# Attention of a four-layer gated block: negated score maxima added by an extra float32r pass

## The reference

```python
q = (target @ Wq.T + bq).reshape(B, L, H, D).transpose(0, 2, 1, 3)   # k, v alike, of the context
q = _apply_rope(q, cos_q, sin_q)
attn = jnp.einsum('bhld,bhkd->bhlk', q, k) * scale
attn = jnp.where(context_mask[:, None, None, :], attn, -jnp.inf)
attn = jax.nn.softmax(attn, axis=-1)
x = jnp.einsum('bhlk,bhkd->bhld', attn, v)
```

## Time and profile before

| | us |
|---|---|
| median of 3 runs | 832.74 (831.04 to 834.12) |
| the profiled execution: its own time | 834.48 |
| its span, first to last instruction | 832.7 |
| mean granted TensorE clock, share of full | 0.932 |
| TensorE matmul busy / weight loads | 694.4 / 413.5 |
| DVE / ACT / POOL busy | 475.5 / 329.4 / 245.0 |
| attention stage, first unit to last copy | 109.30 to 327.71 |

### The profile page before, as it was taken

The page is one execution under the profiler, slowest core; times in us unless marked ns, Lnnn a source line. Parts: engine busy times, 40 slices in busy tenths (PEclk is TensorE's granted clock), DMA queues, the critical chain, the costliest instruction groups (busy, mean ns, idle before and its releaser), DMA issues. The chain is left out here.

```text
span 832.7 us, 10715 instructions
## 1 busy us (share of the span) xinstructions
PE 694.4 (83%) x3613; PEld 413.5 (50%) x3632; DVE 475.5 (57%) x873; ACT 329.4 (40%) x584; POOL 245.0 (29%) x407
## 2 busy tenths in 40 slices
PE   3699869998998997855799999999488999975886
PEld 1377633333333332742455665656355767662554
DVE  3576668888888871643763113121437555456995
ACT  0167626677677676412341111141031120202565
POOL 2356530011011010353050001010103164347797
PEclk9699977999999999885899999999789998996999
DMA  5010000000000001930000000000100000000011
GB/s 186 13 32 25 13 7 0 2 1 0 1 1 1 1 1 71 394 155 0 1 1 0 1 1 0 0 0 1 13 1 0 1 1 1 1 0 0 20 38 45
DMA packets 14104, 21.45 MB, mean 26 GB/s; under 512 B 2160, under 2 KB 11504, under 8 KB 13296
## 3 DMA queue, kind: packets, MB, share of 16 engines
q1 hardware_dynamic: 13200, 20.34, 7.1%
q10 hardware_dynamic: 864, 0.59, 0.2%
HBM read 18.83 MB, written 2.10 MB: 25 GB/s over the span
## 5 line engine op out<-in xcount | busy, mean ns | idle before, releaser
L630 ACT ACTIVATE prob<-ps_s 128x512 f32<-128x512 f32 x256 | 133.9, 600 | 72.3 <-PE ps_s L518 71.6
L562 DVE TENSOR_REDUCE mx<-ps_f 128x2 f32<-128x1024 f32 x128 | 150.0, 1218 | 15.6 <-PE ps_f L498 8.1
L1038 DVE SCALAR_TENSOR_TENSOR qs<-ps_u,wmax,qs 128x512 f32<-128x512 f32 x40 | 29.7, 749 | 113.9 <-ACT qs L1000 113.8
L1000 ACT ACTIVATE qs<-ps_g,wmax 128x512 f32<-128x512 f32 x40 | 27.4, 687 | 144.1 <-PE ps_u L903 144.1
L916 PE MATMUL ps_yE<-down,qs 128*128 128x256 f32 x320 | 77.7, 387 | 7.9 <-DVE qs L1038 6.8
L518 PE MATMUL ps_s<-q_stacks,k_stacks 64*128 64x512 f32 x256 | 75.7, 425 | 10.2 <-ACT prob L630 9.1
L498 PE MATMUL ps_f<-k_stacks,q_stacks 64*128 64x512 f32 x256 | 64.9, 502 | 16.7 <-DVE q_stacks L581 9.7
L916 PEld LDWEIGHTS ps_yE<-down,qs 128*128 128x128 f32 x320 | 61.3, 193 | 22.0 <-DVE qs L1038 9.0
L527 PE MATMUL ps_o<-prob,vst 128*32 128x512 f32 x512 | 69.0, 612 | 0.0
L498 PEld LDWEIGHTS ps_f<-k_stacks,q_stacks 64*128 64x128 f32 x256 | 25.3, 194 | 72.7 <-issue 28.7
L599 POOL COPY vst<-va 128x272 f32<-128x272 f32 x16 | 6.8, 428 | 167.1 <-PE ps_o L527 167.1
(11 more groups left out here) (245 smaller groups left out, 1258.7 us busy)
## 6 DMA issues: line engine op xcount, KB each, us to landing
up<-in_up SPq DMA_DIRECT2D x10, 256.0 KB, 6.7
x<-in_x SPq DMA_DIRECT2D x4, 512.0 KB, 7.9
ctxT<-in_ctxT SPq DMA_DIRECT2D x16, 128.0 KB, 2.0
ks<-in_ctxTC SPq DMA_DIRECT2D x1, 2048.0 KB, 11.9
ks<-in_ctx SPq DMA_DIRECT2D x1, 2048.0 KB, 17.4
out<-x SPq DMA_DIRECT2D x16, 128.0 KB, 1.7
down<-in_down SPq DMA_DIRECT2D x1, 1280.0 KB, 5.7
ks<-in_wqv SPq DMA_DIRECT2D x1, 1024.0 KB, 20.7
```

The costliest lines, as they stand in the source:

```text
L562: dve.tensor_reduce(mx[:, f % 2, qt, 2 * pair:2 * pair + 2], ps_f[n % 2][:, :, :], AX_X, ALU.max).then_inc(used, 1)
L630: act.activation(prob[:, kt % 2, j, :], ps_s[n % 3][:, :], ACT.Exp, scale=SCALE)\
L1038: dve.scalar_tensor_tensor(out=h[:, k % 2, :], in0=ps_u[k % 2][:, :], scalar=wmax[:, 3, order[k], 1:2], in1=sg[:, k % 2, :], op0=ALU.mult, ...
```

## The change

The negated maxima no longer go into the query stack. A step's maxima, transposed, now take a place in the ring of three `ps_s` (a *slot*), and ACT copies them to a new tile `minus` (float32r). `mt` holds two heads' worth of rows: the two pairs of a step share one set of four transposes. Each score gets a pass of its own ahead (`lowered`, now a function of TensorE): a stationary `pick` with ones in the two rows of its pair's maxima, and `minus` as the moving operand, with start=True; the score then accumulates on it. The pass for score j + 1 is issued before score j. The ring counts 17 slots for a step, the maxima's ahead of tile 2. `split` moves from DVE to POOL and becomes three operations. Fourteen units run ahead instead of twelve. DVE keeps only the row maxima.

```diff
-def max_unit(f):
-
-    return UNITS + (UNITS + 1) * f + (MAX_AFTER if f < STEPS - 1 else 0)
-
-
-def score_unit(f, i):
-
-    if f == 0:
-        return i
-    return UNITS + (UNITS + 1) * (f - 1) + i + (1 if i >= MAX_AFTER else 0)
+def score_slot(s, kt, j):
+
+    added = kt // 2 if s + 1 < STEPS else 0
+    return 1 + (QT * G + 1) * s + G * kt + j + added
+
+
+def max_slot(f):
+
+    return score_slot(f - 1, 2, 0) - 1 if f else 0
...
-        mt = sb("mt", [P, 2, QT, G, ROWS], F32)
+        mt = sb("mt", [P, 2, QT, 2, ROWS], F32)
+        minus = sb("minus", [P, 2, S], F32R)
+        pick = sb("pick", [P, 2, P], F32R)
...
-            def first_scores(f, i):
-
-                n = score_unit(f, i)
+            def first_scores(n):
+
                 wait(pe, used, n - 1)
+                f, i = divmod(n, UNITS)
...
             def maxima(f):
 
-                n = max_unit(f)
+                n = max_slot(f)
                 pe.wait_ge(mt_ready, f + 1)
-                wait(pe, used, n - 1)
-                for pair in range(2):
-                    for qt in range(QT):
-                        last = pe.transpose(ps_f[n % 2][:, pair, qt * P:(qt + 1) * P],
-                                            mt[:, f % 2, qt, 2 * pair:2 * pair + 2, :]
-                                            .rearrange("p h r -> p (h r)"), id32)
-                last.then_inc(filled, 1)
+                wait(pe, slot_read, n - 2)
+                for qt in range(QT):
+                    last = pe.transpose(ps_s[n % 3][:, qt * P:(qt + 1) * P],
+                                        mt[:, f % 2, qt, :, :].rearrange("p h r -> p (h r)"), id32)
+                last.then_inc(slot_done, 1)
+
+            def lowered(s, kt, j):
+
+                n = score_slot(s, kt, j)
+                pair, h = divmod(j, 2)
+                if kt == 0 and j == 0:
+                    pe.wait_ge(slot_read, max_slot(s) + 1)
+                wait(pe, slot_read, n - 2)
+                pe.matmul(ps_s[n % 3][:, :], pick[rows(h), pair, :], minus[rows(h), s % 2, :], start=True, stop=False)
 
             def scores(s, kt, j):
-                n = s * 16 + kt * G + j
-                wait(pe, exp_done, n - 2)
+                n = score_slot(s, kt, j)
                 pair, h = divmod(j, 2)
                 pe.matmul(ps_s[n % 3][:, :], ks[rows(h), 2 * s + pair, kt * P:(kt + 1) * P],
-                          qs[rows(h), 2 * s + pair, :], start=True, stop=True).then_inc(s_done, 1)
+                          qs[rows(h), 2 * s + pair, :], start=False, stop=True).then_inc(slot_done, 1)
 
             def values(s, kt):
-                pe.wait_ge(exp_done, s * 16 + kt * G + G)
...
-            for i in range(UNITS):
-                first_scores(0, i)
-            for i in range(MAX_AFTER):
-                first_scores(1, i)
+            for n in range(UNITS + 2):
+                first_scores(n)
             maxima(0)
-            for i in range(MAX_AFTER, 4):
-                first_scores(1, i)
+            for n in range(UNITS + 2, LEAD):
+                first_scores(n)
+            pe.wait_ge(pick_preset, 5)
+            lowered(0, 0, 0)
             for s in range(STEPS):
-                ahead = [(s + 1, i) for i in range(4, UNITS)] + [(s + 2, i) for i in range(4)]
-                pe.wait_ge(used, max_unit(s) + 1)
                 for kt in range(QT):
-                    if kt == QT - 1 and s + 1 < STEPS:
-                        maxima(s + 1)
                     for half in range(2):
-                        f, i = ahead[2 * kt + half]
-                        if f < STEPS:
-                            first_scores(f, i)
+                        ahead = UNITS * s + LEAD + 2 * kt + half
+                        if ahead < UNITS * STEPS:
+                            first_scores(ahead)
+                        if kt == 2 and half == 0 and s + 1 < STEPS:
+                            maxima(s + 1)
                         for j in (2 * half, 2 * half + 1):
+                            then = (s * QT + kt) * G + j + 1
+                            if then < STEPS * QT * G:
+                                lowered(then // (QT * G), then // G % QT, then % G)
                             scores(s, kt, j)
                     if kt:
...
+            for n in range(UNITS * STEPS):
+                f, i = divmod(n, UNITS)
                 qt, pair = divmod(i, 2)
+                if i == 0:
+                    wait(dve, mt_ready, f - 1)
...
 
-            def split(f):
-
-                dve.wait_ge(used, score_unit(f, UNITS - 1) + 1)
-                if f > 1:
-                    dve.wait_ge(filled, max_unit(f - 2) + 1)
-                high, low = mt[:, f % 2, :, :, MAX_ROW], mt[:, f % 2, :, :, MAX_ROW + 1]
-                dve.tensor_scalar(high.bitcast(F32R), mx[:, f % 2, :, :], -1.0, None, ALU.mult).then_inc(mt_half, 1)
-                dve.wait_ge(mt_half, f + 1)
-                dve.scalar_tensor_tensor(out=low, in0=mx[:, f % 2, :, :], scalar=-1.0, in1=high, op0=ALU.mult,
-                                         op1=ALU.subtract).then_inc(mt_ready, 1)
-
-            def lowered(f):
-
-                n = max_unit(f)
-                dve.wait_ge(filled, n + 1)
-                own = qs[:, 2 * f:2 * f + 2, :]
-                dve.tensor_tensor(own, ps_f[n % 2][:, :, :], own.bitcast(F32), ALU.add).then_inc(used, 1)
-            dve.wait_ge(mt_preset, 1)
-            for f in range(STEPS):
-                for i in range(UNITS):
-                    if f and i == MAX_AFTER:
-                        lowered(f - 1)
-                    first_maxima(f, i)
-                split(f)
-            lowered(STEPS - 1)
...
             pool.memset(mt[:, :, :, :, :], 0.0).then_inc(mt_preset, 1)
+            pool.memset(pick[:, :, :].bitcast(F32), 0.0).then_inc(pick_preset, 1)
+            pool.wait_ge(pick_preset, 1)
+            for h in range(2):
+                for pair in range(2):
+                    at = ROWS * h + ROWS // 2 * pair
+                    pool.memset(pick[at:at + 2, pair, :].bitcast(F32), 1.0).then_inc(pick_preset, 1)
+                    pool.wait_ge(pick_preset, 2 + 2 * h + pair)
...
+            def split(f):
+
+                pool.wait_ge(used, UNITS * (f + 1))
+                if f > 1:
+                    pool.wait_ge(slot_done, max_slot(f - 2) + 1)
+                own = mt[:, f % 2, :, :, :].rearrange("p q h (a c) -> p q a h c", a=2)
+                high, low = own[:, :, :, :, 0], own[:, :, :, :, 1]
+                m = mx[:, f % 2, :, :].rearrange("p q (a h) -> p q a h", h=2)
+                pool.tensor_scalar(high.bitcast(F32R), m, -1.0, None, ALU.mult).then_inc(mt_half, 1)
+                pool.wait_ge(mt_half, 2 * f + 1)
+                pool.tensor_tensor(low, m, high, ALU.add).then_inc(mt_half, 1)
+                pool.wait_ge(mt_half, 2 * f + 2)
+                pool.tensor_scalar(low, low, -1.0, None, ALU.mult).then_inc(mt_ready, 1)
...
             pool.wait_ge(bp_in, 16)
+            split(0)
             for s in range(STEPS):
                 if s > 1:
                     stage_values(s, s % 2)
+                if s + 1 < STEPS:
+                    split(s + 1)
                 bias(s)
...
         def _(act):
+            def copy_maxima(f):
+                n = max_slot(f)
+                act.wait_ge(slot_done, n + 1)
+                if f > 1:
+                    act.wait_ge(slot_done, score_slot(f - 2, QT - 1, G - 1) + 1)
+                act.copy(minus[:, f % 2, :], ps_s[n % 3][:, :]).then_inc(slot_read, 1)
+
             def exps(s, kt):
+                wait(act, pv_done, s * QT + kt - 1)
                 for j in range(G):
-                    n = s * 16 + kt * G + j
-                    act.wait_ge(s_done, n + 1)
-                    if j == 0:
-                        wait(act, pv_done, s * QT + kt - 1)
+                    n = score_slot(s, kt, j)
+                    if kt == 2 and j == 0 and s + 1 < STEPS:
+                        copy_maxima(s + 1)
+                    act.wait_ge(slot_done, n + 1)
                     act.activation(prob[:, kt % 2, j, :], ps_s[n % 3][:, :], ACT.Exp, scale=SCALE)\
-                       .then_inc(exp_done, 1)
+                       .then_inc(slot_read, 1)
...
+            copy_maxima(0)
```

More of the change, by code:

```diff
@@ L56 @@
 MAX_ROW, MASK_ROW = 3 * HD, 3 * HD + 2
-UNITS, MAX_AFTER = 2 * QT, 2
+UNITS, LEAD = 2 * QT, 14
 SCALE = HD ** -0.5
@@ L478, in phase_attend @@
         filled, used = sem("filled"), sem("used")
-        mt_preset, mt_half, mt_ready = sem("mt_preset"), sem("mt_half"), sem("mt_ready")
-        s_done, exp_done, pv_done, o_copied = sem("s_done"), sem("exp_done"), sem("pv_done"), sem("o_copied")
+        mt_preset, mt_half, mt_ready, pick_preset = sem("mt_preset"), sem("mt_half"), sem("mt_ready"), sem("pick_preset")
+        slot_done, slot_read, pv_done, o_copied = sem("slot_done"), sem("slot_read"), sem("pv_done"), sem("o_copied")
         v_preset, v_ready = sem("v_preset"), sem("v_ready")
```

(25 more changed lines are left out.)

## The result

| | before | after |
|---|---|---|
| median, us | 831.89 | 878.51 |
| lowest to highest | 830.94 to 834.12 | 877.08 to 880.03 |
| ratio, 95% interval | | 1.0562 (1.0532 to 1.0592) |
| the profiled execution | 834.48 | 877.08 |
| its span | 832.7 | 875.2 |

The medians stand 46.6 apart, the profiled executions 42.6: the profiled one of before (834.48) lies above its four timed ones, that of after is the lowest of its four. The stage grew by 43.9, and the rest of the program, untouched, took 1.4 less in this pair of profiles. So the whole change is in the stage.

What follows compares the result with a forecast made beforehand. It took a loop of waits through ACT and TensorE, DVE outside it, to bound the kernel. Steady steps +32.1, end +4.9 and start -1.9 sum to +35.1, taking the median from 832.74 to 868 us, range 852 to 884.

Steps and rivals of the forecast that it cites:

- 14 steady steps: Attention stage, steady stretch: each step goes from 12.55 to 14.84 us, +32.1 us over 14 steps.
- start of the stage: Before the transposes of step 1: DVE's wait for POOL's zeroing goes, fewer units follow; -1.9 us, between -3 and 0.
- end of the stage: From the transposes of step 15 to the last copy's end: 20.8 us for 15.9, +4.9 us.
- The mechanism: Key tiles: passes hold scores and values one exponential longer; a plain tile's values start at 1.56, +0.49 us a tile.
- hop: Delay between engines: 0.1 us a tile of uncertainty, 6 us each way in the range.
- weights loaded ahead of a held pass: Held pairs on TensorE might start 0.1 us sooner, some 6 us less in all; 0 was taken.
- POOL's split: Three small operations a step on POOL, 0.7 to 2.0 us with hops; cost 0, up to 1 us a step if uncovered.
- The pair of pass and score: On TensorE, opposite row halves overlap, so pass plus score costs what a pair costs now, 0.23 us, not 0.47.
- Serial passes: Rival: pass and score don't overlap on TensorE, 0.47 us together; +30 us, giving 898; chance 6%.
- The clock: Rival: more frequent TensorE waits lower its clock; +48 us if half the tiles ran so, giving 916; chance 3%.
- A held pass that holds nobody: Rival: score 3 and values start while the next tile's pass waits, plain tiles keep 2.83 us; 821; chance 5%.
- No difference: Rival: the hold is partly hidden in time priced as serial, and DVE's relief pays the rest; chance 4%.

Runs made afterwards that it cites:

- b_held: Kernel before with one number changed: each score waits for one exponential more than its buffer asks, no passes; 862.5 us, ratio 1.0379.
- a_nopass: Changed kernel without the 256 pass matmuls, their waits kept on the scores, maxima not taken off; 894.2 and 899.5 us.
- a_ring4: Changed kernel with the first scores' PSUM in three single banks and a fourth place in the scores' ring, all passes kept; 846.6 us, ratio 1.0178.
- a_waits: Changed kernel with three waits put otherwise: ACT asks for values after the score, the maxima's copy not at all, tile 0's pass drops one; 870.4 us, ratio 1.0455.
- a_swap: Changed kernel with score j issued ahead of the pass for score j + 1; 869.5 us, ratio 1.0447.
- a_full: Changed kernel, passes kept, with four-place scores' ring, reordered waits, scores ahead of next passes, values and second unit ahead of fourth score; 832.2 us, ratio 0.9995.

## Why the prediction was right

Forecast 868 with 852 to 884, slower at 91%; measured 878.5, so the rise is 46.6 where 35 was forecast. Term by term, from the two profiles:

| term | predicted | measured |
|---|---|---|
| 14 steady steps | +32.1 | 215.97 - 175.71 = +40.3 |
| start of the stage | -1.9 | 24.26 - 26.77 = -2.5 |
| end of the stage | +4.9 | 22.09 - 15.93 = +6.2 |
| rest of the program | 0 | -1.4 |
| span | +35.1 | +42.5 |

*The mechanism* was right in each place: the hold at 0.65 for the first pass and 1.14 for the second, the values behind it, 1.83 ahead of the maxima. b_held, a_nopass's tiles and a_ring4 tell it from the price of the passes. The longer hold alone is 30 of the 46.6 (b_held). The rest of a step is read from the traces: of 15.41 less 14.31, 0.30 are the second waits (a_waits), and 0.75 the way of the maxima through the scores' ring and ACT, since tiles 1 and 2 together take 8.42 in a_waits and 7.67 in b_held. No run has that way alone, and none has DVE's relief alone; the long idle times of DVE fit the sum, which held no DVE.

*The term that was too small* is the steady step, 14.84 for 15.41 (15.43 by the transposes, with the one long step and the low clock of step 14 in it). Of the 0.57 a step, 0.30 is the second waits of an instruction (a_waits shows it); the text had a "hop" in its range, not in its sum. Another 0.18 is left in tile 1 without them (4.87 for 4.69): the transposes start 0.43 after the unit (225.48 to 225.91) and not 0.33, and ACT's copy 0.69 after them in a_waits, for the 0.62 taken. In the kernel before the transposes came behind values, where no such gap is seen (210.47 to 211.47, the 1.00 that values take). The saving of up to 6 us for weights loaded ahead of a held pass did not come: load and matmul start together at the release (224.05 and 224.06), and the matmul takes 0.50, as from a standing start.

*Start.* The wait for POOL went, as said. *POOL's split* takes 0.27, 0.23 and 0.28, 0.94 from first start to last end and so close to the lower bound. No transpose waits for it. The prediction had nobody waiting for POOL; DVE does, once a step:

```profile
221.99 2.36 DVE L572 TENSOR_REDUCE mx<-ps_f 128x2 f32<-128x1024 f32 x2 [1.11 <-POOL mt L600]
```

This row maximum starts 0.61 after its unit where the one of the tile before starts 0.55 after, and DVE had been idle anyway, so the wait is not on the path. *The pair of pass and score* costs nearly what a pair of scores costs: 0.01 to 0.03 a tile more. *The end* is 1.3 longer than forecast, and 0.7 of it is the low clock at the last transposes: exp 0 comes 1.89 after them (349.37 to 351.26) and 1.22 in the steady part.

*The rivals.* Serial passes: out, they start 0.01 apart. The clock: it held at 1.00 in the steady stretch; but in a_nopass, with the same holds, it fell, and there the Trainium skill's account of a clock that falls with short idles between groups ("TensorE: Matmul & The Clock Gate", "A second HAM failure mode: psum-queue depth-cycling") has its case: granted 0.79 for 80 us. It would have said the same of the changed kernel, and there the trace disagrees. A held pass that holds nobody: out, at 219.46 and 219.47, and by a_swap. No difference: out; a_full gets there, by other means.

## What to carry to other kernels

Work put ahead of an instruction in an in-order queue brings its wait along: ask for each added instruction what it waits for, and what stands behind it that did not wait for that. A producer that runs one place ahead needs one more buffer, or it shortens the ring for everybody. If two waits stand before one instruction, name first the one that comes last.

## What the runs showed of the hardware

- Two 64-row matmuls in opposite halves, one starting an accumulation and one ending another, run side by side (starts 219.46 and 219.47): in this held loop the 256 extra ones cost 0.01 to 0.03 us a tile.
- Such a pair stays in order under a wait: the score, whose own half and buffer were free, started 0.01 after the held pass ahead of it, not before.
- A second wait ahead of an instruction, if it is the late one, costs about 0.06 us each time: -0.30 us a step for five of them (four on ACT, one on TensorE).
- With 256 matmuls left out and the waits kept the kernel was slower: 894.2 and 899.5 for 878.5, at a granted clock of 0.79 from 140 to 220 us where the changed kernel had 1.00.
- Transposes of 128 rows started 0.43 us after a pair of 64-row matmuls, where another such pair starts 0.34 after it (225.48 to 225.91, and 221.38 to 221.72).
